# A new order of TensorE's matmuls in the first attention layer, with the causal mask of the score maxima added by matmuls

## What is computed

```python
Wdkv = x @ latent_w + latent_b
q = jnp.einsum('btc,hcl->bhtl', x, Wd_w) + Wd_b[None, :, None, :]
scores = jnp.einsum('bhtl,bsl->bhts', q, Wdkv) / jnp.asarray(np.sqrt(d_head), dtype=x.dtype)
causal = jnp.tril(jnp.ones((t, t), dtype=bool))
scores = jnp.where(causal[None, None, :, :], scores, -jnp.inf)
attn = jax.nn.softmax(scores, axis=-1)
y = jnp.einsum('bhts,bsl->bhtl', attn, Wdkv)
z = jnp.transpose(y, (0, 2, 1, 3)).reshape(b, t, h * Wdkv.shape[-1])
return z @ out_w + out_b
```

## Time and profile before

| | us |
|---|---|
| median of 3 runs | 1744.3 (1737.26 to 1744.72) |
| profiled execution, own time | 1746.09 |
| its span in the trace | 1744.6 |
| busy in the span: TensorE matmuls | 1504.7 (86%) |
| busy: VectorE | 1146.8 (66%) |
| busy: ScalarE | 997.4 (57%) |
| busy: GpSimd | 920.7 (53%) |

### The profile page before, as it was taken

How to read it: one execution, slowest core, us unless ns; L and a number is a source line. 1 busy time by engine, 2 the same in 40 slices (tenths; PEclk the granted TensorE clock), 3 DMA queues, 4 the chain that set the end, 5 groups by cost and what they waited for, 6 DMA issues and landing times.

```text
span 1744.6 us, 44545 instructions
## 1 busy us (share of the span) xinstructions
PE 1504.7 (86%) x13025; PEld 1078.0 (62%) x13027; DVE 1146.8 (66%) x4175; ACT 997.4 (57%) x2526; POOL 920.7 (53%) x1625
## 2 busy tenths in 40 slices
PE   4798999999999999998997588888888888885883
PEld 4644555555555555546997477777777777764772
DVE  3356655555555555553654498998989989976561
ACT  3344555555555555553332688888888888852341
POOL 5234555554544554553444566666666666632663
PEclk8579999999999999999999699999999999996666
DMA  7402222222222222223332111211112121116444
GB/s 196 134 19 69 56 55 56 56 55 54 55 55 55 55 55 56 56 61 85 69 69 55 23 44 44 45 42 41 44 44 45 42 41 44 44 29 128 84 91 113
DMA packets 240882, 107.55 MB, mean 62 GB/s; under 512 B 145465, under 2 KB 229242, under 8 KB 240762
## 3 DMA queue, kind: packets, MB, share of 16 engines
q1 hardware_dynamic: 230586, 93.23, 22.3%
q0 software_dynamic: 10240, 13.64, 3.7%
HBM read 61.92 MB, written 40.16 MB: 59 GB/s over the span
## 4 chain that ended last, share of the span: by engine, by line
PE 59%; ACT 18%; issue 7%; POOL 6%; DVE 5%; DMA 3%; SPq 1%; POOLq 1%; DVEq 0%; ACTq 0%
PE bankB L1861 7%; PE bankA L1818 6%; PE bankT L1841 5%; PE bankT L1993 4%; PE bankT L1847 3%; PE bankB L1874 3%; PE bankB L1865 3%; ACT qx L1602 3%; ACT km L1611 2%; ACT gqx L1602 2%; PE bankT L2112 2%; PE bankS L1829 2%; ACT probs L1503 2%; PE bankA L2094 2%; ACT rows L1675 2%
## 5 line engine op out<-in xcount | busy, mean ns | idle before, releaser
L653 POOL TENSOR_SCALAR_AFFINE_SELECT probs<-probs 128x512 f32<-128x512 f32 x256 | 176.6, 713 | 225.6 <-ACT probs L1503 225.6
L947 DVE CUSTOM_DVE_ANT_0 masked<-bankS,causal 128x128 bf16<-128x128 f32 x512 | 127.9, 287 | 178.7 <-PE bankS L1831 177.7
L1503 ACT ACTIVATE probs<-bankT 128x1024 f32<-128x1024 f32 x128 | 131.1, 1024 | 134.5 <-PE bankT L1847 134.5
L1498 ACT ACTIVATE qT<-bankA,bd 128x256 f32<-128x256 f32 x256 | 107.5, 471 | 159.3 <-PE bankA L1818 155.6
L950 DVE CUSTOM_DVE_ANT_0 masked<-bankS,causal 128x256 bf16<-128x256 f32 x512 | 195.6, 420 | 0.1
L1818 PE MATMUL bankA<-xnT,wd 128*128 128x256 f32 x512 | 147.2, 411 | 1.9 <-ACT qT L1498 1.9
L1841 PE MATMUL bankT<-qT,kT 37*128 37x512 f32 x512 | 143.4, 637 | 2.4 <-ACT probs L1505 2.2
L1861 PE MATMUL bankB<-probs,vaug 128*64 128x512 f32 x512 | 140.8, 628 | 3.3 <-ACT yT L1510 0.9
L1307 DVE STREAM_TRANSPOSE pt<-pe 128x768 f32<-128x768 f32 x128 | 124.4, 972 | 26.4 <-ACT pe L1588 26.2
L2112 PE MATMUL bankT<-vx,pt 128*64 128x68 f32 x1024 | 72.6, 228 | 55.9 <-ACT gkm L1631 55.9
L1588 ACT ACTIVATE pe<-pr 128x768 f32<-128x768 f32 x128 | 108.0, 844 | 7.2 <-DVE pr L1301 4.8
(11 more groups left out here) (307 smaller groups left out, 4257.1 us busy)
## 6 DMA issues: line engine op xcount, KB each, us to landing
rzb<-reciprocals SPq DMA_DIRECT2D x128, 128.0 KB, 2.6
yT<-yT SPq DMA_DIRECT2D x64, 128.0 KB, 2.3
xtab<-tab SPq DMA_DIRECT2D x32, 192.0 KB, 2.0
xs_sorted<-zeros SPq DMA_DIRECT2D x1, 4608.0 KB, 18.5
qT<-xs_sorted SPq DMA_DIRECT2D x144, 32.0 KB, 1.8
ys_sorted<-qT SPq DMA_DIRECT2D x36, 128.0 KB, 1.9
value_rows<-vrow SPq DMA_DIRECT2D x32, 128.0 KB, 1.8
vx<-value_rows SPq DMA_DIRECT2D x256, 16.0 KB, 1.8
```

The source lines that it names most:

```text
L653: pool.affine_select(out=blocks, in_=blocks, compare_op=ALU.is_ge, fill=0.0, base=0, pattern=[[0, 4], [1, P]], channel_multiplier=-1).then ...
L947: dve.tensor_tensor_reduce(masked[:, e, 0:P], bankS[:, e, 0:P], causal[:, P:2 * P], -1.0, -NEG, ALU.add, ALU.min, mneg[:, n.half, e, j, 0:1])
L1503: act.activation(pT[:, g % 2].rearrange("p e j t -> p e (j t)"), bankT[:, 0:2, :], ACT.Exp, scale=SCALE0).then_inc(S["exp_done"], 1)
```

## The change

The mask comes into the scores of `smax` by four bf16 matmuls a pair, `rowsel` times `rowneg` (64 rows each, 128 columns), which write -1e30 into the blocks on the diagonal before the scores are added; VectorE's `red` becomes two plain reductions. `av` is cut into `av_first` and `av_second`, and `st_ps`, which told ScalarE that both halves of the scores are there, is told after each half, so that the first exponential may begin ahead of `st_second`. `kv` moves to the end of the step and from `bankS` to `bankT`; `qproj` 0 of the next batch moves ahead of `smax` 7. Between any two `smax` stands other work. GpSimd's, VectorE's and ScalarE's steps are put in an order to match, and two of the four DMAs of the maxima go from SP's to ScalarE's queue.

```diff
-        causal = sb("causal", [P, 2 * P])
-        masked = sb("masked", [P, 2, 3 * P], BF16)
+        rowsel = sb("rowsel", [P, 2, P], BF16)
+        rowneg = sb("rowneg", [P, 2, LP], BF16)
...
             def maxima(n):
                 sp.wait_ge(S["mT_sb"], n.b + 1)
-                for k in range(P // W):
+                for k in range(P // W // 2):
...
-            pool.affine_select(out=causal[:, P:2 * P], in_=causal[:, P:2 * P], compare_op=ALU.is_ge, fill=NEG, base=0,
-                               pattern=[[-1, P]], channel_multiplier=1)
+            for e in range(2):
+                r = HALVES[e]
+                pool.affine_select(out=rowsel[r, 0, :], in_=rowsel[r, 0, :], compare_op=ALU.not_equal, fill=1.0, base=0,
+                                   pattern=[[-1, P]], channel_multiplier=1)
...
             def step(b, n, m, rows):
                 if n:
                     round_keys(n)
-                    round_queries(n, 0)
                 if rows == "staged":
                     scatter(b)
...
+                if n:
+                    round_queries(n, 1)
                 clip(b, 0)
                 if n:
-                    round_queries(n, 1)
+                    round_queries(n, 2)
+                clip(b, 1)
...
             def red(n, j):
                 dve.wait_ge(S["s_ps"], n.b * PAIRS + (j + 1))
-                passed(dve)
-                for e in range(2):
-                    dve.tensor_tensor_reduce(masked[:, e, 0:P], bankS[:, e, 0:P], causal[:, P:2 * P], -1.0, -NEG, ALU.add, ALU.min,
-                                             mneg[:, n.half, e, j, 0:1])
...
+                dve.tensor_reduce(mneg[:, n.half, :, j, 0], bankS[:, :, 0:128], AX.X, ALU.max, negate=True)
+                dve.tensor_reduce(mneg[:, n.half, :, j, 1], bankS[:, :, 128:384], AX.X, ALU.max,
+                                  negate=True).then_inc(S["red_done"], 1)
...
             def probs(b, g):
-                act.wait_ge(S["st_ps"], b.b * GROUPS + (g + 1))
+                act.wait_ge(S["st_ps"], b.b * (2 * GROUPS) + (2 * g + 1))
                 act.activation(pT[:, g % 2].rearrange("p e j t -> p e (j t)"), bankT[:, 0:2, :], ACT.Exp,
                                scale=SCALE0).then_inc(S["exp_done"], 1)
+                act.wait_ge(S["st_ps"], b.b * (2 * GROUPS) + (2 * g + 2))
...
                 yevac(b, GROUPS - 1)
-                if m:
-                    qevac(m, 0)
+                if n:
+                    maxima(n)
...
+                for k in range(2):
+                    for e in range(2):
+                        blocks = bankS[:, e, 0:384].rearrange("p (i h c) -> p i h c", h=2, c=LP)[:, 0:3:2, k]
+                        pe.matmul(blocks, rowsel[HALVES[e], k, :], rowneg[HALVES[e], k, :].unsqueeze(1).to_broadcast([LP, 2, LP]),
+                                  start=(k == 0), stop=False, skip_group_check=True)
                 for e in range(2):
-                    pe.matmul(bankS[:, e, 0:P], qb[ROWS[e], j, 0:P], kb[ROWS[e], 0:P], start=True, stop=True, skip_group_check=True)
+                    pe.matmul(bankS[:, e, 0:128], qb[ROWS[e], j, 0:P], kb[ROWS[e], 0:P], start=False, stop=True, skip_group_check=True)
...
-                st_second(b, 0)
-                for g in range(1, GROUPS):
-                    if n:
-                        smax(n, 2 * g - 1)
-                        if g < GROUPS - 1:
-                            qproj(n, g + 1)
-                    st_first(b, g, True)
-                    if n and g < GROUPS - 1:
-                        smax(n, 2 * g)
-                    st_second(b, g)
-                    if n and g == GROUPS - 1:
-                        smax(n, 2 * g)
-                    av(b, g - 1, "ranks" if ranks else q is not None)
+                st_second(b, 0, prior)
+                if n:
+                    smax(n, 1)
+                    qproj(n, 2)
+                st_first(b, 1, True)
+                if n:
+                    smax(n, 2)
+                av_first(b, 0, "ranks" if ranks else q is not None)
+                st_second(b, 1, True)
+                av_second(b, 0)
...
```

More of the change, by code:

```diff
@@ L695, in _ @@
             layer1_masks(3)
+            round_queries(second, 0)
             step(first, second, Batch(1, 0), None)
@@ L1107, in _ @@
             turned(1)
-            kv(first)
+            kv(first, bankS)
             stats0(3)
@@ L1129, in _ @@
             best()
-            kv(second)
+            kv(second, bankS)
             onehot(0)
@@ L1499, in qevac, with maxima @@
                                    bias=bd[:, j:j + 1]).then_inc(S["q_sb"], 1)
+            def maxima(n):
+                act.wait_ge(S["mT_sb"], n.b + 1)
+                for k in range(P // W // 2, P // W):
+                    act.dma_start(qT[L:LP + L + 1:LP, n.half].rearrange("e j (t k q) -> e (j t) k q", t=2, q=W)[:, :, k],
+                                  mT[W * k:W * (k + 1), n.half, :]).then_inc(S[f"m_in{n.half}"], 16)
             def probs(b, g):
-                act.wait_ge(S["st_ps"], b.b * GROUPS + (g + 1))
+                act.wait_ge(S["st_ps"], b.b * (2 * GROUPS) + (2 * g + 1))
                 act.activation(pT[:, g % 2].rearrange("p e j t -> p e (j t)"), bankT[:, 0:2, :], ACT.Exp,
                                scale=SCALE0).then_inc(S["exp_done"], 1)
+                act.wait_ge(S["st_ps"], b.b * (2 * GROUPS) + (2 * g + 2))
                 act.activation(pT1[:, g % 2].rearrange("p e j t -> p e (j t)"), bankT[:, 2:4, 0:T], ACT.Exp,
@@ L1515, in step @@
                         qevac(n, g + 1)
+                    if m and g == GROUPS - 1:
+                        xnt(m)
                     probs(b, g)
@@ L1519, in step @@
                 if m:
-                    xnt(m)
+                    qevac(m, 0)
                 yevac(b, GROUPS - 1)
-                if m:
-                    qevac(m, 0)
+                if n:
+                    maxima(n)
             first, second = Batch(0, 0), Batch(0, 1)
@@ L1548, in _ @@
             xnt(second)
+            maxima(first)
             qevac(second, 0)
@@ L1804, in xnt, with kv @@
                 ins.then_inc(S["xnT_ps"], 1)
-            def kv(n):
+            def kv(n, keys_ps=bankT):
                 u = n.half
                 pe.wait_ge(S["xnT_sb"], n.b + 1)
-                pe.matmul(bankS[:, 0, 0:T], lw[:, :, :].rearrange("p e l -> p (e l)"), xnT[:, u, :], start=True, stop=True)
+                pe.matmul(keys_ps[:, 0, 0:T], lw[:, :, :].rearrange("p e l -> p (e l)"), xnT[:, u, :], start=True, stop=True)
                 for t in range(2):
-                    ins = pe.matmul(bankS[:, 0, T + t * L:T + (t + 1) * L], xnT[:, u, t * P:(t + 1) * P], lwr[:, 0:L], start=True, stop=True)
+                    ins = pe.matmul(keys_ps[:, 0, T + t * L:T + (t + 1) * L], xnT[:, u, t * P:(t + 1) * P], lwr[:, 0:L], start=True, stop=True)
                 ins.then_inc(S["kv_ps"], 1)
@@ L1816, in qproj @@
                     pe.wait_ge(S["q_sb"], n.b * PAIRS + 2 * r)
+                else:
+                    pe.wait_ge(S["xnT_sb"], n.b + 1)
                 for k in range(2):
@@ L1838, in st_first, with st_second @@
                 if prior:
-                    pe.wait_ge(S["exp_done"], b.b * (2 * GROUPS) + 2 * g)
-                for e in range(2):
-                    pe.matmul(bankT[:, e, :], kT[KEYS[e], u, 0:P], qT[KEYS[e], u, 2 * g:2 * g + 2, :].rearrange("p j t -> p (j t)"),
-                              start=True, stop=True, skip_group_check=True)
-            def st_second(b, g):
-                u = b.half
+                    pe.wait_ge(S["exp_done"], b.b * (2 * GROUPS) + (2 * g - 1))
+                for e in range(2):
+                    ins = pe.matmul(bankT[:, e, :], kT[KEYS[e], u, 0:P], qT[KEYS[e], u, 2 * g:2 * g + 2, :].rearrange("p j t -> p (j t)"),
+                                    start=True, stop=True, skip_group_check=True)
+                ins.then_inc(S["st_ps"], 1)
+            def st_second(b, g, prior):
+                u = b.half
+                if prior:
+                    pe.wait_ge(S["exp_done"], b.b * (2 * GROUPS) + 2 * g)
                 for e in range(2):
@@ L1862, in av, with av_second @@
                               start=True, stop=False, skip_group_check=True)
+            def av_second(b, g):
+                u = b.half
                 pe.wait_ge(S["clipped"], b.b * (2 * GROUPS) + (2 * g + 2))
@@ L1894, in step @@
                 if n:
-                    qproj(n, 1)
                     smax(n, 0)
```

77 lines of the change are left out of this document (53 added, 24 removed).

## The result

The changed kernel takes 1780.6 us, the median of four runs (1773.13 to 1790.5); the kernel before takes 1743.43 beside it. The ratio is 1.0223, its 95% interval 1.0179 to 1.0266: slower, by 37 us. The profiled execution of the change is the slowest of its four, 1790.5 us, so times per batch are read from its loop, where the clock is full, and whole times from the medians.

A forecast was written before the change was run, and what follows sets the result against it. TensorE's own work was taken as the bound. Thirty batches at +1.24 us (+37) and +2 for opening and end gave 1785 from the profiled 1746.1, or 1783 against the median; own range 1772 to 1795, overall 1762 to 1806.

The forecast's parts named there:

- Changes of arrangement and laid-open weights (+0.80 and +0.63): TensorE's loop: eight more changes at 0.10 us, +0.80 a batch; weight loads exposed at new arrivals, +0.63.
- rival of hidden loads (1764): TensorE loads the next group's weights during the running one across new changes too; 0.63 us a batch goes; chance 0.10.
- Masks (+1.04): Mask matmuls ahead of each smax, hidden by nothing: two concurrent pairs at 0.065 us, eight times a batch, +1.04 us.
- The sum: Per-batch total of changes, exposed weights, masks and removed waits: 0.80 + 0.63 + 1.04 - 1.23 = +1.24 us.
- dearer masks of the rival (1.5): Masks at 1.5 us a batch if weight loads set the pace, +14 us; chance 0.13, shared with waits that stay.
- Waits (-1.23): Four TensorE waits a batch, at smax 1, 2, 6 and av of group 3, all removed: -1.23 us.
- No slower (1740): The 0.10 us gaps belong to semaphore waits, so added changes and loads cost nothing: -0.19 us a batch; chance 0.05.
- Edits costed at nothing: GpSimd's opening constants, kv at the step's end, half the maxima's DMAs on ScalarE's queue: no cost in the batch sum.
- `kb`'s cover of 0.8 us: With kv at the step's end, outp before smax 0 hides the cast of kT with 0.8 us to spare.
- signs of being wrong: Profile: st_second behind av at 0.43 us, mask pairs at 0.09 or more, or TensorE notes for kb, probs or maxima DMAs.
- Opening and end (+2, 0 to 4): Outside the thirty batches: opening masks at half clock 2.1 us, partly in waits; last step may return 1; together +2.
- the worst of them stood at 1809: Dearer masks (+14 us) and waits that stay (+12 us) both happening: 1809 us; either alone 1797; chance 0.13.

The follow-up runs named there:

- e2_av_whole: Changed kernel with st_second issued ahead of av_first in groups 1 and 2, so av is whole again; 1753.14 us, 1.0055 of the kernel before.
- e4_order_av_whole: Changed kernel with the mask back in VectorE's reduction, no mask matmuls, and av whole again; 1726.13 us, 0.9893 of the kernel before.
- e1_no_mask: Changed kernel without its mask matmuls, maxima taken over unmasked scores; 1748.33 us, 1.0014 of the kernel before.
- e3_order_alone: Changed kernel with the mask back in VectorE's custom reduction and no mask matmuls; 1754.83 us, 1.0061 of the kernel before.
- e6_casts_first: Kernel before, with GpSimd's query casts of pairs 2 to 7 moved ahead of the clips; 1744.61 us, 0.9995 of the kernel before.
- e7_casts_and_invert: Kernel before, with casts ahead of clips and VectorE's reciprocal moved behind pair 1's reduction; 1736.6 us, 0.9933 of the kernel before.

## Why the prediction was right

The forecast was 1783 us, slower; measured were 1780.6. Step by step:

- **Changes of arrangement and laid-open weights (+0.80 and +0.63).** The rows show them at the values assumed, and the price of `av` to `st_second`, which the trace of before did not have, at the upper of its two ends: 0.63 us is 0.43, 0.10 and 0.10. The four changes with their loads that e2_av_whole and e4_order_av_whole took out were put at 4 x 0.10 + 0.22 + 0.10 = 0.72, and measured 0.70 both times. The other four changes were not taken out by themselves. With that the rival of hidden loads (1764) falls. The Trainium skill, page "TensorE: Matmul & The Clock Gate", section "Step-by-step: what each phase is for", says that a load is pulled ahead of running matmuls when the row groups don't conflict or the load goes to the background weight buffer. By that rule the 0.10 us would not stand wherever one of the two holds; the trace has it so from `smax` 0 to `st_first` (0.86), and not across a change.
- **Masks (+1.04).** Mis-sized: 0.91 by e1_no_mask. The sum took two concurrent matmuls at 0.065 us; 0.91 / 16 is 0.057, under even the lower end of 0.06. The dearer masks of the rival (1.5) did not come.
- **Waits (-1.23).** All four are gone, and no new one stands in the loop. If the changes and loads cost the 1.43 of the sum, e3_order_alone (+0.11) makes the waits worth 1.32, 0.09 more. Two omissions make most of these 0.09. The prediction passed over a fifth wait, which no note names, at `st_first` of group 3 in the kernel before (TensorE's and ScalarE's timelines):

```profile
425.32 1.13 PE L1841 MATMUL bankT<-qT,kT 37*128 37x512 f32 x4
```

```profile
424.68 0.59 ACT L1505 ACTIVATE probs<-bankT 128x512 f32<-128x512 f32 x1
```

`smax` 5 starts at 425.09, so `st_first` comes 425.32 - 425.09 - 0.16 = 0.07 late, right behind the exponential that ends at 424.68 + 0.59 = 425.27, and it takes 426.29 - 425.32 = 0.97 instead of 0.86. So 0.11 us of weights stood open behind this wait without a change of arrangement: a load is not always hidden within one. In the change this `st_first` stands behind `xnt`, a new arrival whose load the sum also left out, and takes 427.77 - 426.80 = 0.97. The two omissions come to 0.18 - 0.11 = 0.07 us.

For `smax` 2 the prediction named the cast alone. That its wait went is owed also to `red` of pair 1, which the change moves ahead of the reciprocal (e6_casts_first, e7_casts_and_invert).
- **The sum** was to be +1.24 us a batch and is +1.02; the masks are 0.13 of the 0.22 that are missing, the rest is the 0.09 of the waits.
- **No slower (1740)** falls with e2_av_whole: the gaps go with the changes, while the waits stay. The prediction's own argument against it, that `smax` 4 starts without a gap, was circular, since its 0.97 was read from that same row.
- **Edits costed at nothing.** `kb`'s cover of 0.8 us held in the loop and failed in the first two steps (1.93 and 1.16 us); the prediction had looked at the loop alone. A note for `kb` was one of its signs of being wrong. The wait for `kb` is also in e1_no_mask and e3_order_alone, so it belongs to the order. The maxima's DMAs end no wait of TensorE: from 780 to 1000 us the waits view of the change, with what was waited for, us in total, times and longest, has

```profile
PE bankS L2034 <- DVE probs L1213: 2.7, 2, 1.8
PE bankB L1910 <- ACT yT L1530: 1.6, 2, 0.8
PE bankT L1871 <- ACT probs L1522: 1.4, 1, 1.4
PE bankB L1894 <- ACT yT L1530: 1.0, 2, 0.7
```

- **Opening and end (+2, 0 to 4).** By the medians 37.2 - 30.6 = 6.6 us lie outside the thirty batches, so the forecast's nearness owes something to two errors of opposite sign: the thirty batches cost 6.6 us less than forecast, and what lies around them about 5 more. The interval of the ratio is as wide (31 to 46 us), so this 5 is not firmly measured. The traces say more of the opening. These are the `st_first` of the same group and batch, the ninth of the program, in the kernel before, the change, e1_no_mask and e3_order_alone:

```profile
150.28 1.02 PE L1841 MATMUL bankT<-qT,kT 37*128 37x512 f32 x4
```

```profile
161.51 1.13 PE L1871 MATMUL bankT<-qT,kT 37*128 37x512 f32 x4 [0.37 <-issue]
```

```profile
149.82 1.13 PE L1866 MATMUL bankT<-qT,kT 37*128 37x512 f32 x4
```

```profile
160.60 1.13 PE L1854 MATMUL bankT<-qT,kT 37*128 37x512 f32 x4
```

The change is 11.2 us late there, e2_av_whole (152.24), with the same masks, only 2.0, as much as the forecast put around the batches, and e1_no_mask is 0.5 early. The 3.4 us by which the first `st_first` of the change came late are thus no loss that lasts: e1_no_mask starts its own at 99.40, 3.1 late, and has made it up.

What sets the change and e3_order_alone apart is the stretch in which TensorE's matmuls take nearly double length: in these two it lasts until about 130 us, in all the other traces single lengths are back by 113. By the medians, too, the same two stand apart: they lose 6.6 and 5.9 us outside the thirty batches, the other kernels of the table between -2.7 and +1.7. So the likely cause of the 5 us is this stretch. The prediction had no term for it, and it was luck that it nearly made up for what the batches cost less than forecast. This is an argument from one trace of each kernel, not shown by a run: in e3_order_alone's trace the part behind the attention was shorter in turn (937.8 us from the last `st_first` to the end, 947.0 in e1_no_mask), and why the stretch lasts longer in two kernels stays open.
- **The range.** 1762 to 1806 was said to take in the worse cases, but the worst of them stood at 1809.

## What to carry to other kernels

Where TensorE is the bound and switches between arrangements of its array, count the switches of an order as well as its waits: here an order without a single wait in the loop lost to one with at least 1.23 us of waits a batch, until four of its switches were taken out. Work moved onto the bound engine to relieve another was paid in full here (0.91 us a batch) once the other engine no longer ended a wait, and in part (0.30) while it still did, so try the order first and the relief only if a wait for that engine is left. And an idle note names one releaser only; before a wait is costed as a gain, look at when the next one would have come.

## What the runs showed of the hardware

The clock of the first step was not what I had looked for. In e3_order_alone TensorE's `st_first` took 2.08 us, and the windows view of that stretch gives a granted clock of 1.00:

```profile
104.62 2.08 PE L1854 MATMUL bankT<-qT,kT 37*128 37x512 f32 x4
```

```profile
90.00:100.00 10.00, 7.23 (x22) 4.59 (x23) 4.68 (x23) 1.67 (x5) 1.12 (x3) 1.00 0.01 2
100.00:110.00 10.00, 10.00 (x32) 3.78 (x28) 3.72 (x18) 3.75 (x7) 3.40 (x7) 1.00 0.00 0
```

In the loop the same group takes 1.13. In the change it takes 2.02 us and more where the view gives 0.50, the level of 1.2 GHz. So in e3_order_alone the lengths fit that level while the view gives 1.00, the level of 2.4 GHz, after TensorE had been busy for 7.23 of 10 us; the length of a known group tells more here than that column. In this kernel the double lengths end in a `qproj` that starts at 126.93 us, in e4_order_av_whole, with the same masks on VectorE, in one that starts at 111.00. What ends them was not settled.
